# Row maxima of causal attention: full-height products with zero-padded keys, or 32-row groups of TensorE in bursts of three banks

## The chip, the cores and the metric

One NeuronCore of a Trainium2 chip runs the whole kernel. The metric is device time in microseconds (us) from the first to the last instruction of that core; lower is better. The engines are TensorE (PE; its weight loads are listed as PEld), VectorE (DVE), ScalarE (ACT), GpSimd (POOL) and SyncE (SP), each with its own in-order instruction queue, tied together by semaphores.

## What is computed

A transformer block on 2 sequences of 1024 tokens with width 512: a modulated layer norm, attention with 16 query heads of 32 channels over one shared key and value head, a residual, a second modulated layer norm, and a mixture of 64 experts with 8 chosen per token and a shared expert. Only the attention matters here:

```python
q = rmsnorm(apply_rope((x @ Wq.T).reshape(B, S, H, hd).transpose(0, 2, 1, 3), S), w_qn)
k = rmsnorm(apply_rope(x @ Wk.T, S), w_kn)                      # one key head, hd = 32
scores = jnp.einsum('bhqd,bkd->bhqk', q, k) * scale
scores = jnp.where(causal, scores, jnp.finfo(scores.dtype).min)
attn = jax.nn.softmax(scores, axis=-1)                          # needs each row's maximum
out = jnp.einsum('bhqk,bkd->bhqd', attn, v)
```

## The kernel before

The first half of the span is attention, the second half the experts. Attention goes through 16 tiles of 128 query rows, `t` = 0 to 15, eight to a sequence (`i = t % 8`). Every engine walks the same hand-written calendar: a loop over slots `m`, 16 slots to a tile, in which each stage of the work has a fixed slot (tables `AT`, `FIRST_AT` and so on). Within a slot PE does, in this order, `row_max` (L1082), `scores` (L1132, transposed scores of a 256-query chunk), `values` (L1147, probabilities times values, in 32-column groups of the array, four heads side by side), then stages of other tiles: `stack` (L1117), the projections (L1051, L1060), transposes (L1040, L1072, L1079), the output projection (L1177), router logits and more. DVE does `end_max`, then `row_max`, then the rest of its slot (rotation, splitting, residuals, routing).

The row maxima are a pass of their own: the scores of a tile are made once with "f32r" operands (one pass through the array) only to find each row's maximum, which is then put into the query operand as extra channels (`end_max`, `stack`), so that the exponentials later need no maximum. For tile `i` a head's scores have (i+1)·128 columns. They are cut into pieces, each of which fills one PSUM bank of 512 columns: up to 512 columns `heads_in(width)` heads share a bank (4, 2, 1, 1 heads for i = 0 to 3); over 512 columns each head has a bank of its first 512 columns, and the rest is shared by 4, 2, 1, 1 heads (i = 4 to 7). That makes 4, 8, 16, 16, 20, 24, 32 and 32 banks for i = 0 to 7, 304 over both sequences. Three banks (4, 5, 6) go round; the pieces are spread evenly over the tile's 16 slots.

The contraction is only 32 channels. Before the change, a query operand `qpT` holds four heads stacked on 128 partitions, and the keys stand in `kpad`: four copies, copy `j` non-zero on partitions 32j to 32j+31 alone. So each head is one 128-row product (L1092). The bank that holds the diagonal gets a causal bias through an identity product (L1096). `s_mm` counts finished banks, and DVE reduces each bank when it is there (L1610) and counts it in `s_max`; PE waits before it writes bank n until bank n−3 is reduced. `keys_out` on ACT fills `kpad` with four copies of 32 partitions (L817) after the key transpose (L1079). At the start DVE clears `kpad` (L1489). Full-array products of ones (L1032, `keep_warm`) fill some early gaps.

Of the kernel before, what the change touches and what calls it, by code (L numbers as in the profile page):

```python
# [6 lines left out]
H, HD = 16, 32  # L7
# [52 lines left out]
def build_program(nc, x, c_t, wmod, wq_t, wkv_t, wo_t, w_pre, w_qn, w_kn, router_t, e_bias,  # L60
# [11 lines left out]
    with ctx:  # L72
# [27 lines left out]


        att = ExitStack()
        kpad = sb(att, "kpad", [P, GH, S], f32r)
        qs = sb(att, "qs", [P, 2, H, QK])
        wq = sb(att, "wq", [P, KC, D])
        wkv = sb(att, "wkv", [P, KC, 2 * HD])
# [70 lines left out]
        nmax = sb(att, "nmax", [P, 2, H])  # L177
        seen = sb(att, "seen", [P, E])
        seen_b = sb(att, "seen_b", [P, E], bf16)
        steps = sb(att, "steps", [P, P, 4], f16)  # L180
# [169 lines left out]

            return min(GH, 512 // width)

        def pieces(i):

            width = (i + 1) * P
            if width <= 512:
                return H // heads_in(width)
            return H + H // heads_in(width - 512)

        def pieces_before(t):  # L360

            return sum(pieces(k % TPB) for k in range(t))

        def pieces_at(i, h):
            width = (i + 1) * P
            if width <= 512:
                k = heads_in(width)
                return [(h // k, h, k, 0, width)] if h % k == 0 else []
            k = heads_in(width - 512)
            found = [(h + h // k, h, 1, 0, 512)]  # L370
            if h % k == k - 1:
                found.append((h + h // k + 1, h + 1 - k, k, 512, width))
            return found

        def max_view(n, heads, width):

            bank = ps[:, MAX_BANK + n % MAX_BANKS, :].rearrange("p (a k) -> p a k", a=heads)
            return bank[:, :, 0:width]

        def keys(q):  # L380

# [145 lines left out]
        def _(sp):  # L527
# [51 lines left out]

            for t in range(CT * CLOSE):  # L580
                if t == CT * (CLOSE - 1):
                    sp.wait_ge(s_mm, pieces_before(NT))
# [160 lines left out]
        def _(act):  # L743
# [58 lines left out]
            def pack_out(t):  # L802
                act.wait_ge(s_pack, t + 1)
                if t >= 2:
                    act.wait_ge(s_mm, pieces_before(t - 1))
                act.activation(qpT[:, t % 2, :, :], ps[:, T_BANK, :].rearrange("p (g t) -> p g t", t=P), ACT.Copy)\
                   .then_inc(s_qp, 1)

            def keys_out(t):
                b, i = divmod(t, TPB)  # L810
                act.wait_ge(s_pack_k, t + 1)
                act.activation(kT[0:QK, b, i * P:i * P + P], ps[0:QK, T_BANK, 0:P], ACT.Copy)
                if t and i == 0:
                    act.wait_ge(s_mm, pieces_before(t))
                for j in range(GH):
                    r = slice(HD * j, HD * j + HD)
                    last = act.activation(kpad[r, j, i * P:i * P + P], ps[0:HD, T_BANK, 0:P], ACT.Copy)  # L817
                last.then_inc(s_packT, 1)

            def stack_out(t, q4):  # L820
# [207 lines left out]
        def _(pe):  # L1028
# [47 lines left out]
            def pack_keys(t):  # L1076
                keep_warm(("pack_keys", t))
                pe.wait_ge(s_qp, t + 1)
                pe.transpose(ps[0:QK, T_BANK, 0:P], ks[:, :], ident).then_inc(s_pack_k, 1)  # L1079

            def row_max(t, h):
                i = t % TPB  # L1082
                for n, first, heads, lo, hi in pieces_at(i, h):
                    if n == 0:
                        keep_warm(("row_max", t))
                        pe.wait_ge(s_packT, t + 1)
                    n += pieces_before(t)
                    if n >= MAX_BANKS:
                        pe.wait_ge(s_max, n - MAX_BANKS + 1)
                    view, diagonal = max_view(n, heads, hi - lo), hi == (i + 1) * P  # L1090
                    for a in range(heads):
# [28 lines left out]
            def scores(q, g, kt):  # L1120
                b, off, n = q // CPB, first_query(q, kt), step_of(q, g, kt)
                if g == 0 and kt == 0:
                    pe.wait_ge(s_qT, CT * (q + 1) * NG)
                for pr in range(2):
                    if wide_units(2 * n + pr) >= 4:
                        pe.wait_ge(s_exp, 2 * n + pr - 3)
                    elif wide_units(2 * n + pr) >= 2:
                        pe.wait_ge(s_max, pieces_before(NT))
# [356 lines left out]
        def _(dve):  # L1485

            dve.memset(ones_b[:, :], 1.0).then_inc(s_blank, 1)
            dve.memset(silu_c[:, :, :], 0.0).then_inc(s_blank, 1)
            dve.memset(kpad[:, :, :].bitcast(f32), 0.0)  # L1489
            dve.memset(ones[:, :], 1.0)  # L1490
            dve.memset(mhalf[:, :], -0.5)
            dve.memset(seen[:, :], 0.0)
# [89 lines left out]
            def split(t, n):  # L1582
# [30 lines left out]
            def end_max(t):  # L1613
                q_parts = qs[:, t % 2, :, :]
                dve.drain()
                if t % TPB >= 4:
                    dve.tensor_tensor(nmax[:, 0, :], nmax[:, 0, :], nmax[:, 1, :], ALU.min)
                    dve.drain()
                dve.tensor_copy(q_parts[:, :, 3 * HD].bitcast(f32r), nmax[:, 0, :])
                dve.drain()  # L1620
                dve.tensor_tensor(q_parts[:, :, 3 * HD + 1].bitcast(f32r), nmax[:, 0, :], q_parts[:, :, 3 * HD],
                                  ALU.subtract).then_inc(s_nmax, 1)
                dve.drain()

            def divide(q, g):
# [480 lines left out]
```

## Time and profile before

| | |
|---|---|
| time, median of 3 runs (lowest to highest) | 1232.77 us (1232.52 to 1236.47) |
| profiled execution, its own span | 1233.0 us |
| PE busy | 1168.1 us, 95% |
| DVE busy | 972.6 us, 79% |
| ACT busy | 762.0 us, 62% |
| POOL busy | 497.9 us, 40% |
| DVE maxima, L1610 | 304 instructions, 191.3 us |
| PE products of the maxima, L1092 | 384 instructions, 146.7 us |

Busy time is the union of an engine's instructions. A product's listed duration has the time in it that results need to leave the array, so that a chain of products overlaps itself: the rate is read from start to start, not from the mean duration. "PEclk" in the views of stretches is the clock granted to TensorE, as a share of full speed.

### The profile page before, as it was taken

How to read it: one execution, taken by the hardware profiler on the slowest of the kernel's cores; microseconds unless marked ns; L12 is line 12 of the kernel's file. 1: busy time of each engine (PE TensorE's matmuls, PEld its weight loads, DVE VectorE, ACT ScalarE, POOL GpSimd, SP SyncE). 2: the span in 40 equal slices, each digit the busy share in tenths (PEclk: the TensorE clock that was granted, in tenths of full speed). 3: DMA queues.
4: the chain of work that ended last, by engine and by line, in shares of the span. 5: the costliest groups of instructions: out<-in, count | busy, mean ns of one | idle time of the engine just before them, and what ended most of it. 6: DMA issues, size and time to landing. Idle time of an engine off the chain costs nothing.

```text
span 1233.0 us, 25541 instructions
## 1 busy us (share of the span) xinstructions
PE 1168.1 (95%) x8905; PEld 879.7 (71%) x8905; DVE 972.6 (79%) x1881; ACT 762.0 (62%) x1507; POOL 497.9 (40%) x375
## 2 busy tenths in 40 slices
PE   8988999999999988999999999999999999999996
PEld 4455556555565655555557899999999999999982
DVE  4678776756657888775767889899888999999976
ACT  3456555555664644455564477787777887777841
POOL 1122212102122111201100148887888778788740
PEclk9999999989999998999999999999999999999999
DMA  9570000000000000003004179999999999999988
GB/s 349 172 302 1 2 18 2 10 9 2 15 10 10 9 1 22 1 10 95 29 14 141 25 225 299 289 302 302 292 295 306 299 297 296 298 301 294 298 231 290
DMA packets 75167, 189.95 MB, mean 154 GB/s; under 512 B 11544, under 2 KB 12184, under 8 KB 74832
## 3 DMA queue, kind: packets, MB, share of 16 engines
q1 hardware_dynamic: 44704, 116.27, 28.0%
q0 software_dynamic: 28672, 71.32, 23.5%
q10 hardware_dynamic: 1712, 1.32, 0.3%
q8 instruction: 48, 0.79, 0.3%
q14 instruction: 31, 0.25, 0.1%
HBM read 136.36 MB, written 52.51 MB: 153 GB/s over the span
## 4 chain that ended last, share of the span: by engine, by line
PE 71%; DVE 13%; DVEq 4%; issue 3%; DMA 3%; ACT 3%; POOL 0%; SPq 0%; POOLq 0%; ACTq 0%
PE ps L1328 22%; PE ps L1367 12%; PE ps L1147 8%; PE ps L1314 5%; PE ps L1177 4%; PE ps L1132 4%; PE ps L1060 4%; PE ps L1092 4%; DVE nmax L1610 3%; PE ps L1117 2%; DMA acc_dram<-y,slots 1%; PE ps L1032 1%; PE ps L1164 1%; DMA wq<-in_wq_t 1%; PE ps L1195 1%
## 5 line engine op out<-in xcount | busy, mean ns | idle before, releaser
L730 POOL DMA_INDIRECT acc_dram<-y,slots x128 | 252.2, 1971 | 74.1 <-issue 47.9
L1610 DVE TENSOR_REDUCE nmax<-ps 128x1 f32<-128x512 f32 (+3 forms) x304 | 191.3, 656 | 95.3 <-PE ps L1096 52.4
L839 ACT ACTIVATE probs<-ps 128x512 f32<-128x512 f32 (+1 forms) x320 | 159.0, 554 | 87.2 <-PE ps L1132 86.3
L681 POOL TENSOR_SCALAR_AFFINE_SELECT probs<-probs 128x512 f32<-128x512 f32 x64 | 44.3, 691 | 376.7 <-ACT probs L839 376.6
L715 POOL DMA_INDIRECT xg<-h_dram,slots x128 | 130.7, 1021 | 84.4 <-DVE slots L1801 40.5
L1092 PE MATMUL ps<-kpad,qpT 128*128 128x512 f32 (+3 forms) x384 | 146.7, 450 | 15.5 <-DVE nmax L1610 13.4
L1328 PE MATMUL ps<-x_hi,e_gu_hi 128*112 128x256 f32 (+1 forms) x768 | 120.1, 278 | 0.0
L1132 PE MATMUL ps<-qT,kT 98*128 98x512 f32 (+1 forms) x320 | 115.1, 437 | 5.0 <-ACT probs L839 4.8
L1328 PE MATMUL ps<-x_hi,e_gu_lo 128*112 128x256 f32 (+1 forms) x768 | 119.6, 278 | 0.0
L1812 DVE TENSOR_TENSOR e_gu_lo<-e_gu,e_gu_hi 128x1408 fp32r<-128x1408 f32 x64 | 103.8, 1622 | 11.0 <-ACT e_gu_hi L960 9.9
L1328 PE MATMUL ps<-x_lo,e_gu_hi 128*112 128x256 f32 (+1 forms) x768 | 109.9, 279 | 0.0
L1328 PEld LDWEIGHTS ps<-x_hi,e_gu_hi 128*112 128x112 f32 (+1 forms) x768 | 105.7, 179 | 5.9
L1092 PEld LDWEIGHTS ps<-kpad,qpT 128*128 128x128 f32 x384 | 67.3, 195 | 50.3 <-DVE nmax L1610 25.4
L1328 PEld LDWEIGHTS ps<-x_hi,e_gu_lo 128*112 128x112 f32 (+1 forms) x768 | 100.8, 179 | 0.0
L1328 PEld LDWEIGHTS ps<-x_lo,e_gu_hi 128*112 128x112 f32 (+1 forms) x768 | 96.0, 179 | 0.0
L1812 DVE TENSOR_TENSOR x_lo<-ps,x_hi 128x1024 fp32r<-128x1024 f32 x72 | 88.1, 1224 | 2.9 <-ACT x_hi L937 1.9
L960 ACT ACTIVATE e_gu_hi<-e_gu 128x1408 fp32r<-128x1408 f32 x64 | 88.2, 1378 | 0.1
L1367 PE MATMUL ps<-e_d_hi,hid_hi 112*128 112x512 f32 (+1 forms) x256 | 85.9, 417 | 0.0
L937 ACT ACTIVATE x_hi<-ps 128x1024 fp32r<-128x1024 f32 x72 | 73.9, 1026 | 18.5 <-PE ps L1314 18.1
L1147 PE MATMUL ps<-probs,v_sb 128*32 128x256 f32 (+1 forms) x1280 | 83.4, 380 | 0.6 <-POOL probs L681 0.6
L1367 PE MATMUL ps<-e_d_hi,hid_lo 112*128 112x512 f32 (+1 forms) x256 | 80.8, 397 | 0.0
L1147 PE MATMUL ps<-probs,ones 128*32 128x256 f32 (+1 forms) x1280 | 79.4, 367 | 0.0
(238 smaller groups left out, 2375.1 us busy)
## 6 DMA issues: line engine op xcount, KB each, us to landing
e_gu<-in_gate_up SPq DMA_DIRECT2D x64, 704.0 KB, 7.3
e_d<-in_w_down SPq DMA_DIRECT2D x64, 224.0 KB, 4.7
acc_dram<-h SPq DMA_DIRECT2D x2, 4608.0 KB, 26.0
e_d<-in_w_down SPq DMA_DIRECT2D x64, 128.0 KB, 5.4
wmod_b<-in_wmod SPq DMA_DIRECT2D x2, 2048.0 KB, 22.0
xg<-h_dram SPq DMA_DIRECT2D x16, 256.0 KB, 7.0
acc_a<-acc_dram SPq DMA_DIRECT2D x8, 512.0 KB, 10.0
acc_b<-acc_dram SPq DMA_DIRECT2D x8, 512.0 KB, 7.7
```

Of the source, the lines that this page charges most:

```text
L715: pool.indirect_dma_start(out=xg[r][:, h, :], out_offset=None, in_=h2_dram, in_offset=bass.IndirectOffsetOnAxis(ap=slots[:, at:at + 1], ax ...
L730: pool.indirect_dma_start(out=acc_dram[a], out_offset=bass.IndirectOffsetOnAxis(ap=slots[:, at:at + 1], axis=0), in_=y[e % 2][:, h, :], in ...
L839: act.activation(probs[:, n % PROBS, 2 * pr:2 * pr + 2, off:CW], unit_bank(2 * n + pr)[:, :, off:CW], ACT.Exp).then_inc(s_exp, 1)
L937: act.activation(x_hi[p][:, :, :].rearrange(flat), pair(0).rearrange(flat), ACT.Copy).then_inc(s_xa, 1)
L960: act.activation(e_gu_hi[p][:, :, :].rearrange(flat), e_gu[p][:, :, :].rearrange(flat), ACT.Copy)\
L1092: last = pe.matmul(view[:, a, :], qpT[:, t % 2, (first + a) // GH, :], kpad[:, (first + a) % GH, lo:hi], start=(a == 0), stop=(a == heads ...
L1132: pe.matmul(unit_bank(2 * n + pr)[:, :, off:CW], kT[0:QK, b, kt * P:kt * P + P], qT[q % 2][0:QK, head:head + 2, off:CW], start=True, stop= ...
L1147: last = pe.matmul(ps[HD * j:HD * j + HD, PV_BANK, at + off:at + CW], v_sb[:, b, kt, :] if at == 0 else ones[:, :], probs[:, (n + kt % 2) ...
L1328: last = pe.matmul(dst, w[:, cc, col:col + wide], rows_t[:, cc, :], start=(k == 0 and cc == 0), stop=(k == 2 and cc == KC - 1))
L1367: last = pe.matmul(ps[:, 6 + h, :], left[:, h * P:(h + 1) * P], w, start=(k == 0), stop=(k == len(products) - 1))
L1610: dve.tensor_reduce(nmax[:, 1 if lo else 0, first:first + heads], max_view(n, heads, hi - lo), AX.X, ALU.max, negate=True).then_inc(s_max, 1)
L1812: return dve.tensor_tensor(dst[:, :, :].rearrange(flat), whole[:, :, :].rearrange(flat), hi[:, :, :].bitcast(f32).rearrange(flat), ALU.sub ...
```

## The change

The keys are now one tile `kq`, with the 32 key channels repeated on all four groups of 32 partitions. DVE writes four copies of the keys side by side into `ks4`, and a second 128-column transpose turns them, so that ACT moves them with one copy of 128 partitions in place of four of 32. A head's product takes only its own 32 rows of `qpT` and `kq`. A bank now holds heads with the same place `j` in their group of four, so that neighbouring banks use different row groups. Banks are handled in bursts of three: PE issues the first head of each of the three banks, then the second heads, and so on, then the diagonal biases of the three, and counts `s_mm` once for the burst. DVE waits for the burst, and then reduces and counts each bank by itself. Before PE writes bank k of a burst, it waits until the bank in the same place has been reduced (`drained`). Tiles i = 0 to 7 have 2, 3, 6, 6, 7, 8, 11 and 11 bursts (54 to a sequence, 108 in all); burst n of N stands in the first slot h with h ≥ 16·n/N, rounded down: for 11 bursts these are slots 0, 1, 2, 4, 5, 7, 8, 10, 11, 13 and 14. The clearing of `kpad` is gone. All waits that counted pieces now count bursts (PE's progress) or banks (DVE's).

```diff
-        kpad = sb(att, "kpad", [P, GH, S], f32r)
+        kq = sb(att, "kq", [P, S], f32r)
+        ks4 = sb(att, "ks4", [P, GH, HD])
...
+        def max_banks(i):
+            found = []
+            for part, (lo, hi) in enumerate(max_parts(i)):
+                k = heads_in(hi - lo)
+                for n in range(H // k):
+                    q, j = divmod(n, GH)
+                    found.append((part * H + n * k, [GH * (q * k + a) + j for a in range(k)], lo, hi))
             return found
+        def bursts(i):
+            banks = max_banks(i)
+            return [banks[n:n + MAX_BANKS] for n in range(0, len(banks), MAX_BANKS)]
+        def bursts_at(i, h):
+            found = bursts(i)
+            return [(n, banks) for n, banks in enumerate(found) if n * H // len(found) == h]
...
 keys_out (ACT):
-                for j in range(GH):
-                    r = slice(HD * j, HD * j + HD)
-                    last = act.activation(kpad[r, j, i * P:i * P + P], ps[0:HD, T_BANK, 0:P], ACT.Copy)
+                last = act.activation(kq[:, i * P:i * P + P], ps[:, T_BANK, P:2 * P], ACT.Copy)
...
 pack_keys (PE):
+                pe.transpose(ps[:, T_BANK, P:2 * P], ks4[:, :, :].rearrange("p j d -> p (j d)"), ident)\
+                  .then_inc(s_pack_k, 1)
...
 row_max (PE):
-                for n, first, heads, lo, hi in pieces_at(i, h):
+                for n, banks in bursts_at(i, h):
                     if n == 0:
                         keep_warm(("row_max", t))
                         pe.wait_ge(s_packT, t + 1)
-                    n += pieces_before(t)
-                    if n >= MAX_BANKS:
-                        pe.wait_ge(s_max, n - MAX_BANKS + 1)
-                    view, diagonal = max_view(n, heads, hi - lo), hi == (i + 1) * P
-                    for a in range(heads):
-                        last = pe.matmul(view[:, a, :], qpT[:, t % 2, (first + a) // GH, :],
-                                         kpad[:, (first + a) % GH, lo:hi], start=(a == 0),
-                                         stop=(a == heads - 1 and not diagonal))
-                    if diagonal:
-                        last = pe.matmul(view[:, :, hi - lo - P:hi - lo], ident_b[:, :],
-                                         bias_b[:, :].unsqueeze(1).to_broadcast([P, heads, P]), start=False, stop=True)
+                    for a in range(max(len(heads) for _, heads, _, _ in banks)):
+                        for k, (_, heads, lo, hi) in enumerate(banks):
+                            if a < len(heads):
+                                if a == 0 and drained(t, n, k):
+                                    pe.wait_ge(s_max, drained(t, n, k))
+                                g, j = divmod(heads[a], GH)
+                                r = slice(HD * j, HD * j + HD)
+                                last = pe.matmul(max_view(k, 1, hi - lo)[:, a, :], qpT[r, t % 2, g, :], kq[r, lo:hi],
+                                                 start=(a == 0), stop=(a == len(heads) - 1 and hi != (i + 1) * P))
+                    for k, (_, heads, lo, hi) in enumerate(banks):
+                        if hi == (i + 1) * P:
+                            last = pe.matmul(max_view(k, 1, hi - lo)[:, :, hi - lo - P:hi - lo], ident_b[:, :],
+                                             bias_b[:, :].unsqueeze(1).to_broadcast([P, len(heads), P]), start=False, stop=True)
                     last.then_inc(s_mm, 1)
...
-            dve.memset(kpad[:, :, :].bitcast(f32), 0.0)
...
 split (DVE):
+                    dve.tensor_copy(ks4[:, :, :].bitcast(f32r), t1[:, H, :].unsqueeze(1).to_broadcast([P, GH, HD]))
...
 row_max (DVE):
-                for n, first, heads, lo, hi in pieces_at(i, h):
-                    n += pieces_before(t)
-                    dve.wait_ge(s_mm, n + 1)
-                    dve.tensor_reduce(nmax[:, 1 if lo else 0, first:first + heads], max_view(n, heads, hi - lo), AX.X, ALU.max,
-                                      negate=True).then_inc(s_max, 1)
+                for n, banks in bursts_at(i, h):
+                    dve.wait_ge(s_mm, bursts_before(t) + n + 1)
+                    for k, (first, heads, lo, hi) in enumerate(banks):
+                        dve.tensor_reduce(nmax[:, first:first + len(heads)], max_view(k, 1, hi - lo), AX.X, ALU.max,
+                                          negate=True).then_inc(s_max, 1)
```

`end_max` reads the maxima in their new order of heads; it has the same three small operations.

## Rows read from the trace of the kernel before

**Rows 1.** The page's busy line and its chain that ended last.
```profile
PE 1168.1 (95%) x8905; PEld 879.7 (71%) x8905; DVE 972.6 (79%) x1881; ACT 762.0 (62%) x1507; POOL 497.9 (40%) x375
...
PE 71%; DVE 13%; DVEq 4%; issue 3%; DMA 3%; ACT 3%; POOL 0%; SPq 0%; POOLq 0%; ACTq 0%
```

**Rows 2.** Stretches: length; busy (instructions) of PE, PEld, DVE, ACT, POOL; PEclk, DMA, GB/s.
```profile
93.00:182.00 89.00, 80.83 (x602) 51.17 (x600) 70.42 (x142) 49.03 (x117) 20.58 (x20) 0.96 0.02 7
182.00:267.00 85.00, 80.57 (x634) 49.16 (x635) 59.62 (x120) 44.37 (x102) 13.38 (x13) 0.94 0.02 7
...
386.00:491.00 105.00, 93.30 (x686) 58.66 (x684) 93.07 (x214) 50.97 (x120) 20.13 (x19) 0.97 0.04 12
491.00:567.00 76.00, 71.88 (x610) 43.26 (x608) 59.63 (x123) 39.72 (x84) 10.05 (x12) 0.98 0.03 9
```

**Rows 3.** Groups by line: busy, mean ns; idle before them, and releasers.
```profile
L1610 DVE TENSOR_REDUCE nmax<-ps 128x1 f32<-128x512 f32 (+3 forms) x304 | 191.3, 656 | 95.3 <-PE ps L1096 52.4 <-PE ps L1092 40.1 <-issue 0.8
```

**Rows 4.** Who waited for whom, PE alone, 30 to 600 us: total, times, longest.
```profile
PE ps L1092 <- DVE nmax L1610: 13.4, 18, 1.8
...
PE ps L1117 <- DVE qs L1621: 4.1, 10, 0.9
PE ps L1092 <- ACT kpad L817: 1.8, 4, 1.0
```

**Rows 5.** Order of time in tile 7: start, length, engine, line, operation.
```profile
241.45 0.60 PE L1189 MATMUL ps<-con,h 128*128 128x128 f32 x4
...
241.81 0.71 PE L1092 MATMUL ps<-kpad,qpT 128*128 128x512 f32 x2
...
242.36 0.23 PE L1096 MATMUL ps<-bias_b,ident_b 128*128 128x128 bf16 x1
242.37 0.31 PEld L1132 LDWEIGHTS ps<-qT,kT 98*128 98x128 f32 x2
242.40 0.71 PE L1132 MATMUL ps<-qT,kT 98*128 98x512 f32 x2
```

**Rows 6.** Order of time: narrow products of tile 0, and a run of L1032.
```profile
39.73 0.52 PEld L1092 LDWEIGHTS ps<-kpad,qpT 128*128 128x128 f32 x4 [0.84 <-issue]
...
35.55 1.67 PE L1032 MATMUL ps<-ones_b 128*128 128x512 bf16 x7
```

**Rows 7.** Order of time: from full array to 32-column groups and back.
```profile
244.28 0.23 PE L1096 MATMUL ps<-bias_b,ident_b 128*128 128x128 bf16 x1
244.44 0.59 PEld L1147 LDWEIGHTS ps<-probs,v_sb 128*32 128x32 f32 x16
244.45 1.07 PE L1147 MATMUL ps<-probs,v_sb 128*32 128x256 f32 x16
...
245.33 1.05 PE L1147 MATMUL ps<-probs,ones 128*32 128x256 f32 x16
...
246.31 0.30 PEld L1060 LDWEIGHTS ps<-wq,hT 128*128 128x128 f32 x2 [0.41 <-issue]
```

**Rows 8.** Order of time: a wait for a bank, and values at the lower clock.
```profile
227.77 0.68 DVE L1610 TENSOR_REDUCE nmax<-ps 128x1 f32<-128x512 f32 x1
227.91 0.19 PEld L1092 LDWEIGHTS ps<-kpad,qpT 128*128 128x128 f32 x1 [1.81 <-DVE nmax L1610]
...
231.48 1.94 PE L1147 MATMUL ps<-probs,v_sb 128*32 128x256 f32 x16
...
233.19 1.27 PE L1147 MATMUL ps<-probs,ones 128*32 128x256 f32 x16
```

**Rows 9.** Stretches, columns as in rows 2, at two falls of the clock.
```profile
223.40:226.80 3.40, 3.01 (x30) 1.81 (x19) 3.00 (x7) 1.79 (x4) 0.35 (x1) 1.00 0.00 0
226.80:230.20 3.40, 1.82 (x10) 1.21 (x10) 3.40 (x8) 1.71 (x4) 0.38 (x2) 1.00 0.00 0
230.20:233.60 3.40, 3.40 (x24) 1.75 (x28) 3.21 (x6) 0.89 (x3) 1.90 (x3) 0.51 0.02 5
...
499.90:503.30 3.40, 1.85 (x13) 1.30 (x12) 3.21 (x7) 1.22 (x4) 2.95 (x2) 1.00 0.00 0
503.30:506.70 3.40, 3.40 (x28) 1.76 (x31) 1.94 (x5) 1.69 (x3) 0.89 (x1) 0.50 0.00 0
```

**Rows 10.** Order of time: key copies of tile 0, clearing of `kpad`, first load.
```profile
35.92 1.08 ACT L817 ACTIVATE kpad<-ps 32x128 fp32r<-32x128 f32 x4
...
2.00 3.47 DVE L1489 MEMSET kpad<- 128x4096 f32 x1 [0.80 <-issue]
...
2.80 13.23 DMA wq<-in_wq_t
```

More of the change, by code:

```diff
@@ L102, in build_program @@
         att = ExitStack()
-        kpad = sb(att, "kpad", [P, GH, S], f32r)
+        kq = sb(att, "kq", [P, S], f32r)
+        ks4 = sb(att, "ks4", [P, GH, HD])
+        hole = sb(att, "hole", [P, (GH - 1) * S - GH * HD])
         qs = sb(att, "qs", [P, 2, H, QK])
@@ L176, in build_program @@
         rr = sb(att, "rr", [P, H + 1])
-        nmax = sb(att, "nmax", [P, 2, H])
+        nmax = sb(att, "nmax", [P, 2 * H])
         seen = sb(att, "seen", [P, E])
@@ L351, in heads_in, with max_parts @@
             return min(GH, 512 // width)
-        def pieces(i):
+        def max_parts(i):
             width = (i + 1) * P
[L356 to L372, printed above, removed]
-            return found
@@ L375, in max_view @@
-        def max_view(n, heads, width):
-            bank = ps[:, MAX_BANK + n % MAX_BANKS, :].rearrange("p (a k) -> p a k", a=heads)
-            return bank[:, :, 0:width]
+            return [(lo, min(width, lo + 512)) for lo in range(0, width, 512)]
+        def max_banks(i):
[5 more added lines that the diff above has]
+                    found.append((part * H + n * k, [GH * (q * k + a) + j for a in range(k)], lo, hi))
+            return found
@@ new lines, in bursts, with bursts_before, banks_before, drained @@
+        def bursts(i):
+            banks = max_banks(i)
+            return [banks[n:n + MAX_BANKS] for n in range(0, len(banks), MAX_BANKS)]
+        def bursts_before(t):
+            return sum(len(bursts(k % TPB)) for k in range(t))
+        def banks_before(t):
+            return sum(len(max_banks(k % TPB)) for k in range(t))
+        def drained(t, n, k):
+            sizes = [len(burst) for s in range(t + 1) for burst in bursts(s % TPB)[:n if s == t else None]]
+            while sizes and sizes[-1] <= k:
+                sizes.pop()
+            return sum(sizes[:-1]) + k + 1 if sizes else 0
@@ new lines, in bursts_at, with by_head, max_view @@
+        def bursts_at(i, h):
+            found = bursts(i)
+            return [(n, banks) for n, banks in enumerate(found) if n * H // len(found) == h]
+        def by_head(flat, width):
+            k = heads_in(width)
+            return flat.rearrange("p (q j a) -> p q a j", j=GH, a=k)
+        def max_view(bank, count, width):
+            heads = heads_in(width)
+            return ps[:, MAX_BANK + bank:MAX_BANK + bank + count, :].rearrange("p b (a k) -> p (b a) k", a=heads)[:, :, 0:width]
@@ L581, in _ @@
                 if t == CT * (CLOSE - 1):
-                    sp.wait_ge(s_mm, pieces_before(NT))
+                    sp.wait_ge(s_mm, bursts_before(NT))
                     sp.wait_ge(s_sc, 2 * steps_before(CLOSE))
@@ L804, in pack_out @@
                 if t >= 2:
-                    act.wait_ge(s_mm, pieces_before(t - 1))
+                    act.wait_ge(s_mm, bursts_before(t - 1))
                 act.activation(qpT[:, t % 2, :, :], ps[:, T_BANK, :].rearrange("p (g t) -> p g t", t=P), ACT.Copy)\
@@ L813, in keys_out @@
                 if t and i == 0:
-                    act.wait_ge(s_mm, pieces_before(t))
-                for j in range(GH):
-                    r = slice(HD * j, HD * j + HD)
-                    last = act.activation(kpad[r, j, i * P:i * P + P], ps[0:HD, T_BANK, 0:P], ACT.Copy)
+                    act.wait_ge(s_mm, bursts_before(t))
+                last = act.activation(kq[:, i * P:i * P + P], ps[:, T_BANK, P:2 * P], ACT.Copy)
                 last.then_inc(s_packT, 1)
@@ L1078, in pack_keys @@
                 pe.wait_ge(s_qp, t + 1)
-                pe.transpose(ps[0:QK, T_BANK, 0:P], ks[:, :], ident).then_inc(s_pack_k, 1)
+                pe.transpose(ps[0:QK, T_BANK, 0:P], ks[:, :], ident)
+                pe.transpose(ps[:, T_BANK, P:2 * P], ks4[:, :, :].rearrange("p j d -> p (j d)"), ident)\
+                  .then_inc(s_pack_k, 1)
             def row_max(t, h):
                 i = t % TPB
-                for n, first, heads, lo, hi in pieces_at(i, h):
+                for n, banks in bursts_at(i, h):
                     if n == 0:
@@ L1127, in scores @@
                     elif wide_units(2 * n + pr) >= 2:
-                        pe.wait_ge(s_max, pieces_before(NT))
+                        pe.wait_ge(s_max, banks_before(NT))
                     elif 2 * n + pr >= 2:
@@ L1606, in row_max @@
                 i = t % TPB
-                for n, first, heads, lo, hi in pieces_at(i, h):
-                    n += pieces_before(t)
-                    dve.wait_ge(s_mm, n + 1)
-                    dve.tensor_reduce(nmax[:, 1 if lo else 0, first:first + heads], max_view(n, heads, hi - lo), AX.X, ALU.max,
-                                      negate=True).then_inc(s_max, 1)
+                for n, banks in bursts_at(i, h):
[3 more added lines that the diff above has]
+                                          negate=True).then_inc(s_max, 1)
             def end_max(t):
+                i = t % TPB
                 q_parts = qs[:, t % 2, :, :]
                 dve.drain()
-                if t % TPB >= 4:
-                    dve.tensor_tensor(nmax[:, 0, :], nmax[:, 0, :], nmax[:, 1, :], ALU.min)
+                (lo, hi), *rest = max_parts(i)
+                top = by_head(nmax[:, 0:H], hi - lo)
+                for lo, hi in rest:
+                    dve.tensor_tensor(top, top, by_head(nmax[:, H:2 * H], hi - lo), ALU.min)
                     dve.drain()
-                dve.tensor_copy(q_parts[:, :, 3 * HD].bitcast(f32r), nmax[:, 0, :])
+                columns = [q_parts[:, :, 3 * HD + n].rearrange("p (q a j) -> p q a j", a=top.shape[2], j=GH) for n in range(2)]
+                dve.tensor_copy(columns[0].bitcast(f32r), top)
                 dve.drain()
-                dve.tensor_tensor(q_parts[:, :, 3 * HD + 1].bitcast(f32r), nmax[:, 0, :], q_parts[:, :, 3 * HD],
-                                  ALU.subtract).then_inc(s_nmax, 1)
+                dve.tensor_tensor(columns[1].bitcast(f32r), top, columns[0], ALU.subtract).then_inc(s_nmax, 1)
                 dve.drain()
```

## The prediction, written before the changed kernel was run

> **What bounds the kernel now.** I read the page first. TensorE is busy 95% of the span, VectorE 79%, and the chain that ended last lies on PE for 71% and on DVE for 13% [rows 1]. The expert half is untouched by the diff, so I looked only at attention, tile by tile, in the view of stretches. In tiles 3 to 5, 6 and 7, and 14 and 15 PE is busy nine tenths of the time or more and DVE seven to eight tenths; in tiles 11 to 13 both stand at 89% (93.3 and 93.1 of 105 us) [rows 2]. So PE's own in-order queue sets the pace, with DVE close behind in one stretch of 105 us. The reader should hold that against the DVE group of the maxima: it sat idle 95 us waiting for PE's banks [rows 3], whereas PE itself stood still for a reduced bank 13.4 us [rows 4]. Time taken off PE is worth nearly its full length; time taken off DVE is worth little; any new wait of PE costs its full length, because scores, values and projections of all other tiles queue behind it. The median of the runs, 1232.77, and the profiled span, 1233.0, are the same within 0.3 us, so I sum against 1233. About 0.3% (3.7 us) is what a measurement of this kernel can tell from no change.
>
> **Part 1, the products themselves.** Column time first. A head of tile i streams (i+1)·128 columns: 36·128·16·2 = 147,456 columns. Seven products of 512 columns take 1.67 us with a tail of about 0.38, so 0.215 us each [rows 6]; the column time is 62 us. Three at a time would make it 21, if products in different row groups run side by side. No row of before shows row groups. The nearest row shows column groups: 16 products of L1147 start at 244.45 and the next 16 at 245.33, 0.055 us apiece, where each one alone has 256 columns in two passes, 0.215 us: four do run together [rows 7]. I take the same for row groups.
>
> But the same rows show the price of changing the split of the array. Without a change, the weights of L1132 begin to load as the bias product starts (242.37 against 242.36) [rows 5]. With one, the weights for L1147 wait 0.16 us after the bias product starts (244.44 against 244.28), and on the way back those for L1060 start only at 246.31, when the last values product, of 245.33 + 1.05 = 246.38, has all but ended [rows 7]. A full-width weight load takes 0.11 us ((0.52 − 0.19)/3) [rows 6], and it no longer hides behind the product before. I put entering a burst at 0.20 us, leaving it for the short bf16 load of the bias at 0.11, and leaving it for a full-width load (bursts without a diagonal) at 0.20.
>
> Now per three banks, on PE's queue. Before: in tile 7 two banks, one with a diagonal, take 242.40 − 241.81 = 0.59 us [rows 5]; I split that as 0.22 without and 0.37 with the diagonal, the bias costing more than its 0.05 because the next weight load is exposed. Three banks are 0.65 and 1.08. For 384 columns with a diagonal 0.90, for two heads of 256 about 1.03, for four heads of 128 (weight loads of 0.11 each, then a 0.22 bias) 1.98. After: 0.20 + 0.23 + 0.20 = 0.64 without a diagonal; 0.20 + 0.23 + 0.11 + three biases of 0.055 + 0.08 exposed load = 0.80 with one; 0.75, 0.90 and 1.43 for the other three. With the number of banks (4, 8, 16, 16, 20, 24, 32, 32) that is 46 us before and 39.5 after for one sequence, so **−13 us** for both. The changes of split eat most of the 41 that the overlap would give. Bounds: no price for a change of split at all, 108·0.35 = 38 us more gain, −51; no overlap at all, +41, so +28. I stay at −13, nearest to what L1147 shows.
>
> The Trainium skill, TensorEngine Tiling (Array Packing), Key Properties, says that changing the tiling mode drains the TensorE while changing the tile does not; that speaks against this change, and the L1147 rows agree with it (0.16 us to the next weights where it is otherwise 0.01). The same page under Theoretical Speedup allows up to 4× for contractions of 32 rows; by that alone the part would be −41 us, not −13.
>
> **Part 2, keys.** ACT's four copies take 1.08 us [rows 10], one takes about 0.28; but PE stood waiting on them only 1.8 us in all [rows 4], with as much again in weight loads: −3. The second transpose adds 16 products of about 0.11 us on PE: +2. The extra copy on DVE, about 0.2 us × 16, lies in DVE's idle time, except in tiles 11 to 13, where it costs 0.6 at most. The clearing of `kpad`, 3.47 us from 2.00, ends at 5.5 us while the chain waits for the `wq` load until 16 us [rows 10]: nothing. Together **−1** (−4 to +2).
>
> **Part 3, end of a tile.** The last burst stands in slot 13 or 14, before the change the last bank stood in 14 or 15, so `end_max` no longer comes right behind two maxima. PE waits 4.1 us for it now at L1117 [rows 4], more with the weight loads: **−4** (−10 to 0).
>
> **Part 4, the new wait.** Before, PE could fill bank n while n−1 and n−2 were still to be reduced. Now the third bank of a burst needs the third maximum of the burst before. Behind PE's wait stand the slot's scores and values. After the burst's last product 0.25 us pass until DVE has its count, then three maxima of 0.68 [rows 8]: the last bank is free 2.3 us or more later. With two or more slots between bursts PE has 3.5 us or more of other work and does not notice. In tiles 6, 7, 14 and 15, 11 bursts stand in 16 slots and six of the ten steps are to the very next slot. Slots last 85/32 = 2.6 and 76/32 = 2.4 us there [rows 2]; less 0.6 for the burst PE has 1.8 to 2.0 us, so it waits 0.3 to 0.5, and more where DVE has other work in front: the wait of 1.8 us at 227.91 is such a one [rows 8]. 24 such steps at 0.6: **+15** (0 to +30). DVE's other results come up to 1.4 us later behind a block of three maxima; the slack of the calendar hides that, except in tiles 2, 3 and 11 to 13, and this is in the upper bound.
>
> **Part 5, the clock.** The granted clock falls to 1.2 GHz now and then: 0.96, 0.94, 0.97 and 0.98 in the mean of the stretches of rows 2, which is 3.6 + 5.1 + 3.2 + 1.5 = 13 us of clock, or some eight falls as long as the one shown. Ahead of the two shown PE was thinly used: 1.82 us busy of 3.40, then 0.51 of full speed; 1.85 of 3.40, then 0.50 [rows 9]. A fall costs: 16 values products need 1.71 us (231.48 to 233.19) [rows 8] against 0.88 [rows 7], half the length of a fall, so up to 1.7 us, some of which is spent waiting anyway: 1.3. The change takes two thirds of the maxima's column time off PE without shortening the tile by as much, in just the tiles where the clock already falls. I estimate one further fall for each of the ten tiles 2 to 7 and 12 to 15, **+14** (0 to +35).
>
> **Sum.** −13 − 1 − 4 + 15 + 14 = +11: 1233 + 11 = **1244 us**.
>
> **The rivals.** *Faster: the overlap counts and the clock holds.* If the lower clock does not come more often, because PE is fed as densely as now, and the waits in adjacent slots lie in DVE's idle 95 us, the sum is −13 − 1 − 4 + 3 = −15, 1218. If changing to row groups is also somewhat cheaper than to column groups, up to 10 us more go, 1208. For it speak the high share of PE in every stretch and DVE's idle time; against it the falls that are there already. Chance 0.25, for 1208 to 1229.
>
> *Much faster: row groups overlap in full and changing to them is free.* The column time falls by 41 us, and with parts 2 to 4 the time is 1233 − 41 − 5 + 15 = 1202; L1147's two gaps speak against it. Chance 0.08. The skill's speedup rule, taken alone, would end here.
>
> *No difference.* Waits and falls half as dear as I put them: −18 + 15, within 1229 to 1237. Chance 0.15.
>
> *Much slower: row groups do not run side by side*, or the waits compound because DVE, at 89% in tiles 11 to 13, becomes the bound and idles once per burst for PE's 0.9 us refill. Without overlap 41 us come back and the clock falls no oftener: 1233 + 28 − 5 + 15 = 1271. With compounding, 21 bursts × 0.9 = 19 us on top of 1244, 1263. Against the first speaks L1147; against the second that DVE has other work between bursts that covers a refill. Chance 0.10 beyond 1262.
>
> **How the numbers follow.** The forecast, slower by several us up to 1262, has 0.42; faster 0.25 and much faster 0.08; same 0.15; much slower 0.10. The sign turns on parts 4 and 5 being 18 us together. Range: from 1208, leaving out the case in which changes of split are free, to 1268, leaving out the dearest part of the last rival. The forecast's own range is 1237 to 1262. Chances: faster 0.33, same 0.15, slower 0.52.
>
> **What the profile after would show.** Right: products of different row groups starting a few ns apart; gaps of about 0.2 us in weight loads on entering a burst; the busy time of L1092's successor well under 100 us; more stretches at 0.5 of the clock in tiles 2 to 7 and 12 to 15; waits of PE on L1610's successor above the 13.4 of now, mostly in tiles 6, 7, 14 and 15; DVE's idle time ahead of the maxima still near 90. Wrong: no more falls than now (part 5 goes, and the result is about 1230), weight loads of a row group starting before the previous split's products end (part 1 is −40), or waits that stay where they are.

## The result, and the profile after

The changed kernel takes 1246.29 us (median, 1243.51 to 1250.71), 1.0116 of the kernel before (95% interval 1.0088 to 1.0144): 13.7 us slower, where 11 were forecast. The profiled execution spans 1241.8 us and is the fastest of the four runs.

The page after, busy line and chain, in answer to rows 1:

```profile
PE 1174.5 (95%) x8921; PEld 858.8 (69%) x8921; DVE 968.9 (78%) x1896; ACT 745.3 (60%) x1459; POOL 493.3 (40%) x375
...
PE 74%; DVE 13%; ACT 3%; DVEq 3%; issue 3%; DMA 2%; POOL 0%; SPq 0%; POOLq 0%; ACTq 0%
```

Still a TensorE kernel. The stretches of the same tiles (3 to 5, 6 and 7, 11 to 13, 14 and 15; columns as in rows 2):

```profile
94.00:185.00 91.00, 82.22 (x605) 47.22 (x605) 69.17 (x143) 46.36 (x107) 20.22 (x20) 0.89 0.01 4
185.00:270.00 85.00, 82.02 (x648) 44.56 (x646) 60.04 (x124) 43.08 (x98) 13.24 (x13) 0.96 0.02 7
...
385.00:495.00 110.00, 95.88 (x703) 55.12 (x702) 93.45 (x216) 50.59 (x115) 20.84 (x20) 0.94 0.03 9
495.00:576.00 81.00, 75.67 (x606) 41.52 (x607) 60.23 (x123) 35.67 (x76) 10.04 (x12) 0.90 0.02 8
```

Against [rows 2] the last two are longer by 5 us each and the first by 2, and the clock column is lower in three of four: 0.89 for 0.96, 0.94 for 0.97, 0.90 for 0.98.

The maxima's groups of instructions (busy, mean ns; idle before, releasers), of the changed kernel:

```profile
L1637 DVE TENSOR_REDUCE nmax<-ps 128x1 f32<-128x512 f32 (+3 forms) x304 | 183.0, 655 | 97.5 <-PE ps L1123 78.9 <-PE ps L1119 17.7
L1119 PE MATMUL ps<-kq,qpT 32*128 32x512 f32 (+3 forms) x384 | 75.4, 436 | 10.3 <-DVE nmax L1637 7.2 <-ACT kq L840 0.5
```

The products' busy time is 75 us where it was 147, and DVE's idle time stays at 98 (95 in [rows 3]). One burst in order of time, PE's products and then its weight loads, in answer to rows 5 and 7:

```profile
253.99 0.72 PE L1222 MATMUL ps<-rw,h2T 128*128 128x64 f32 x5
254.64 0.50 PE L1119 MATMUL ps<-kq,qpT 32*128 32x512 f32 x3
255.07 0.34 PE L1123 MATMUL ps<-bias_b,ident_b 128*128 128x128 bf16 x3
255.22 0.71 PE L1159 MATMUL ps<-qT,kT 98*128 98x512 f32 x2
...
254.64 0.19 PEld L1119 LDWEIGHTS ps<-kq,qpT 32*128 32x128 f32 x3
255.07 0.17 PEld L1123 LDWEIGHTS ps<-bias_b,ident_b 128*128 128x128 bf16 x3 [0.25 <-issue]
```

Three products of 512 columns take 0.50 us together, where two at full height took 0.71 [rows 5]: row groups do run side by side, and their three weight loads do too (0.19 for three). And the split is paid for: the weights of L1119 start only at 254.64, when the router's products are nearly through (253.99 + 0.72 = 254.71), those of the bias at 255.07, when the burst is (254.64 + 0.50 = 255.14). From 254.64 to L1159 it is 0.58 us; with the 0.2 of the entry, which lies ahead of 254.64, that is close to the 0.80 of the sum.

Who waited for whom, weight loads only (38 to 640 us), before and then after; a weight load shows waits that the tail of the product before hides in PE's own line. Each line has total, times and longest:

```profile
PEld ps L1092 <- DVE nmax L1610: 25.4, 47, 1.9
PEld ps L1117 <- ACT qT L828: 12.3, 26, 0.8
PEld ps L1117 <- DVE qs L1621: 8.2, 11, 1.3
...
```

```profile
PEld ps L1119 <- DVE nmax L1637: 31.6, 67, 3.2
PEld ps L1144 <- ACT qT L851: 19.8, 25, 1.4
PEld ps L1144 <- DVE qs L1652: 2.2, 3, 1.6
```

The wait for the maxima grew by 6 us, the wait for the query parts shrank by 6, and a wait the prediction did not have grew by 7.5: the stack products for ACT's query copy. PE's own line has 7.2 us for the maxima, where it had 13.4 [rows 4]. The weight loads' wait for the maxima in tiles 6 and 7, then 14 and 15, before and then after:

```profile
PEld ps L1092 <- DVE nmax L1610: 5.3, 12, 1.8
...
PEld ps L1092 <- DVE nmax L1610: 5.4, 12, 1.9
```

```profile
PEld ps L1119 <- DVE nmax L1637: 8.1, 19, 0.8
...
PEld ps L1119 <- DVE nmax L1637: 10.1, 25, 1.0
```

So 7.5 us came in the four tiles that part 4 named, in the weight loads; PE's own waits there fell by 3. In order of time, changed kernel, tile 3:

```profile
98.29 0.60 ACT L851 ACTIVATE qT<-ps 98x512 fp32r<-98x512 f32 x1
98.94 0.28 PEld L1144 LDWEIGHTS ps<-con,qs 128*98 128x98 f32 x3 [0.94 <-ACT qT L851]
```

A tile's query is stacked in four steps in four successive slots, and each needs ACT's 0.60 us copy of the step before. Before the change a bank or two of maxima stood in most slots and could cover the copy; now some slots have none. That this is what made the wait longer is not shown: an experiment below with one bank to a burst has most of the growth too.

Last, the clock over the whole span, before and then after:

```profile
core 0: 1233.0 us, clock 0.984
```

```profile
core 0: 1241.8 us, clock 0.971
```

The clock is full or half in every stretch that the trace records, so the time at half is 2 × (1 − clock) × span: 39 us before and 72 after in the profiled executions. A single execution says little here, as every run has its own clock: over the four runs of the changed kernel it is 72, 77, 80 and 97 us, mean 82; over 35 runs of the kernel before it is 25 to 44, mean 34. In the mean it is 48 us more.

### The profile page after: what moved, and what is told of

Same layout as the page of the kernel before. It is cut to its first block, busy times and chain, and to the rows that moved or that the text cites. A ratio compares the mean times of both kernels' runs of the same rounds, so it can differ in the third digit from the quotient of the medians.

```text
span 1241.8 us, 25540 instructions
## 1 busy us (share of the span) xinstructions
PE 1174.5 (95%) x8921; PEld 858.8 (69%) x8921; DVE 968.9 (78%) x1896; ACT 745.3 (60%) x1459; POOL 493.3 (40%) x375
## 4 chain that ended last, share of the span: by engine, by line
PE 74%; DVE 13%; ACT 3%; DVEq 3%; issue 3%; DMA 2%; POOL 0%; SPq 0%; POOLq 0%; ACTq 0%
PE ps L1355 22%; PE ps L1394 12%; PE ps L1174 8%; PE ps L1341 5%; PE ps L1083 4%; PE ps L1159 4%; PE ps L1204 4%; PE ps L1119 4%; DVE nmax L1637 4%; PE ps L1144 2%; PE ps L1123 1%; PE ps L1055 1%; ACT probs L862 1%; DMA wq<-in_wq_t 1%; PE ps L1074 1%
## 5 line engine op out<-in xcount | busy, mean ns | idle before, releaser
L755 POOL DMA_INDIRECT acc_dram<-y,slots x128 | 248.4, 1940 | 77.0 <-issue 51.3
L1637 DVE TENSOR_REDUCE nmax<-ps 128x1 f32<-128x512 f32 (+3 forms) x304 | 183.0, 655 | 97.5 <-PE ps L1123 78.9
L1159 PE MATMUL ps<-qT,kT 98*128 98x512 f32 (+1 forms) x320 | 121.2, 456 | 5.1 <-ACT probs L862 4.7
L1119 PE MATMUL ps<-kq,qpT 32*128 32x512 f32 (+3 forms) x384 | 75.4, 436 | 10.3 <-DVE nmax L1637 7.2
L1174 PE MATMUL ps<-probs,ones 128*32 128x256 f32 (+1 forms) x1280 | 83.7, 382 | 0.0
L1159 PEld LDWEIGHTS ps<-qT,kT 98*128 98x128 f32 x320 | 53.5, 196 | 38.5 <-ACT probs L862 20.5
```

What stands on the lines that cost most here:

```text
L755: pool.indirect_dma_start(out=acc_dram[a], out_offset=bass.IndirectOffsetOnAxis(ap=slots[:, at:at + 1], axis=0), in_=y[e % 2][:, h, :], in ...
L1119: last = pe.matmul(max_view(k, 1, hi - lo)[:, a, :], qpT[r, t % 2, g, :], kq[r, lo:hi], start=(a == 0), stop=(a == len(heads) - 1 and hi ! ...
L1174: last = pe.matmul(ps[HD * j:HD * j + HD, PV_BANK, at + off:at + CW], v_sb[:, b, kt, :] if at == 0 else ones[:, :], probs[:, (n + kt % 2) ...
L1637: dve.tensor_reduce(nmax[:, first:first + len(heads)], max_view(k, 1, hi - lo), AX.X, ALU.max, negate=True).then_inc(s_max, 1)
```

## Experiments

Each is compared with the kernel before on the same chip (medians 1231.0 to 1232.4 us). Two experiments that ran on different chips are best compared by their ratios. "Half" is the time at half clock worked out as above, in the mean of a kernel's runs; lines of the profile show one run.

**Bundling, with full-height products.**

```diff
 (changed kernel)
-   pe.matmul(max_view(k, 1, hi - lo)[:, a, :], qpT[r, t % 2, g, :], kq[r, lo:hi], ...)
+   pe.matmul(max_view(k, 1, hi - lo)[:, a, :], qpT[:, t % 2, g, :], kpad[:, j, lo:hi], ...)
```

> Bursts of three banks with their counts and waits, but full-height products on zero-padded keys and the old way of copying keys, so row groups, the second transpose and their effect on the clock are undone. My sum (waits +15, earlier end of a tile -4): 1244 us, stretches at half clock about as long in all as before (31 us in attention). Rival, the waits cost nothing and the whole loss is row groups and clock: 1229 to 1233 us.

The old key copies are back too. Measured: 1249.19 us, ratio 1.0141 (1.0124 to 1.0158), half 49 us. That is 5 above my 1244 and far from the rival. Bursts of three with their new order of banks cost 17 us, and the changed kernel is 3 us better than this one, with 32 us more at half clock. Its weight loads:

```profile
PEld ps L1116 <- DVE nmax L1634: 29.8, 75, 3.0
PEld ps L1141 <- ACT qT L851: 20.0, 24, 1.3
PEld ps L1141 <- DVE qs L1649: 3.2, 2, 1.7
```

The three waits of the changed kernel are all here, so they come from bundling and order and not from row groups.

**Two and one to a burst,** full height, going round the three banks:

```diff
-   return [banks[n:n + MAX_BANKS] for n in range(0, len(banks), MAX_BANKS)]
+   return [banks[n:n + BURST] for n in range(0, len(banks), BURST)]     # BURST 2, 1
...
-   pe.wait_ge(s_max, drained(t, n, k))
+   pe.wait_ge(s_max, ring(t, n, k) - MAX_BANKS + 1)
```

> As e1_full (full-height products, no row groups), but bursts of two banks that go round the three banks, so that PE may fill a third bank while two wait. If the 17 us of e1_full come from bundling three banks (PE's other work is left bare in the slots without a burst, and PE and DVE are tied tighter), two to a burst should lose less than half: 1235 to 1241 us, and PE's wait at the stack products for ACT's query copy falls from 12 us towards the 5 of before. Rival, they come from the new order of heads or from counting at all: 1246 to 1250 us as before.

> As e5_full2 with one bank to a burst: only the order of heads and banks differs from the kernel before. Bundling theory: 1229 to 1236 us. Rival, the order of heads and banks costs: 1240 us or more.

Measured: 1240.82 us for two (1.0074, 1.0052 to 1.0096), 1233.83 for one (1.0030, 1.0013 to 1.0047). Both lie in my ranges. So one, two and three to a burst cost 3, 10 and 17 us over the kernel before: 14 of the 17 are bundling, about 3 the new order of heads and banks. The stack products' wait for ACT is 17.6, 19.5 and 20.0 us, against 12.3 before: 5.3 of its 7.5 us come with the new order, and it does not fall as expected; it alone is not the cause. Half is 31 us with one and 32 with two, so the 7 us between them are not the clock. What grows from one to two is the wait for the maxima (first one to a burst, then two):

```profile
PEld ps L1121 <- DVE nmax L1639: 23.5, 46, 2.1
```

```profile
PEld ps L1121 <- DVE nmax L1639: 38.9, 56, 3.0
```

From two to three it falls back to 29.8 while the time rises by 8 us. Half rises from 32 to 49 us, which at the price found below (0.34 us of time for each us at half clock) is about 6 of the 8; the rest I can't assign to one wait.

**Row groups in bursts of two.** The same edit on the changed kernel.

> The changed kernel with 32-row groups, but bursts of two in a ring of three banks: 152 in place of 108 changes to row groups and only two products side by side. By my prices of a change of split (0.20 in, 0.11 or 0.20 out) row groups then cost 8 us of PE per sequence more than full height, and the clock some 7: e5_full2 + 22, about 1260 us. Rival, a change of split is cheap: row groups are no dearer than full height, within 5 us of e5_full2.

Measured: 1270.70 us, 1.0327 (1.0304 to 1.0351), 30 us above the same bursts at full height.

```profile
core 0: 1267.1 us, clock 0.956
```

Half is 114 us against 32. The time is 10 us above the 1260 I expected, and the split between causes did not hold: at 0.34 the 82 us more at half clock are 28 of the 30. That leaves some 2 us for row groups in pairs at an even clock, where I had put 16.

**No overlap.** Banks sorted by row group within a tile, so that a burst's banks mostly share one.

```diff
+   found.sort(key=lambda bank: (bank[2], bank[1][0] % GH))
    return found
```

> The changed kernel, with the banks of a tile ordered so that those of one burst mostly have the same row group and can't run side by side; changes of split, waits and column count are the same. If the overlap is worth its 41 us of column time on PE's queue: 1246 + 41 less some falls of the clock that no longer happen, 1273 to 1287 us. Rival, the bursts stand in time that PE waits anyway: under 1262 us.

Measured: 1269.05 us, 1.0305 (1.0285 to 1.0324), 23 us above the changed kernel. Below what I expected and above the rival. One error was mine: 16 banks in bursts of three are not all of one group (14 steps where 6 would do, not 16), so the column time lost is about 28 us, not 41. Half is 84 us against 82, so the clock has no part in it. Most of the 28 shows in the time: the overlap is real and lies on PE's path.

**The price of a change of split.** Full-height bursts with one small 32-row product ahead of each.

```diff
+   if a == 0 and k == 0:
+       pe.matmul(ps[:, MAX_BANK, 0:64], qpT[0:HD, t % 2, 0, :], kpad[0:HD, 0, 0:64], start=True, stop=True)
```

> As e1_full, with one 32-row product of 64 columns ahead of each of the 108 bursts, written into the burst's first bank and overwritten: it adds two changes of split to a burst and next to no column time. By my prices 0.2 + 0.2 + 0.03 us each, 108 times, less what lies in waits: 1249 + 30 to 46, 1279 to 1295 us. Rival, a change of split costs only the weight load of 0.11 us: 1260 to 1265 us.

Measured: 1274.80 us, 1.0357 (1.0297 to 1.0417), 26 us above bursts without it, at the same half (47 and 49 us): 0.24 us for two changes and the small product itself. Between the two theories; the load alone would have made 11 to 16. The weight loads of the small product and of the burst wait for the maxima for 17.7 and 7.7 us, where they waited 29.8 without it:

```profile
PEld ps L1116 <- DVE nmax L1637: 17.7, 28, 2.6
...
PEld ps L1119 <- DVE nmax L1637: 7.7, 27, 0.4
```

So some 4 us, 0.04 to a burst, are seen to be hidden in these waits. That makes 0.28, not the 0.40 of my price; whether more is hidden in other waits is open.

**Products of ones ahead of the bursts** of tiles 4 to 7 and 12 to 15 (74 bursts), after the wait for the burst's first bank; in the changed kernel, in full-height bursts, and two of them in the changed kernel.

```diff
+   if a == 0 and k == 0 and i >= 4:
+       pe.matmul(ps[:, MAX_BANK, :]..., ones_b[:, :], ones_b..., start=True, stop=True)
```

> The changed kernel, with one full-array product of ones (512 columns) ahead of each burst in tiles 4 to 7 and 12 to 15, written into the burst's first bank once it is free and overwritten by the burst. 74 products of 0.22 us and an exposed weight load, 16 to 20 us of PE. If falls of the clock come from a thinly used array and cost 14 us: half-clock time goes from about 61 us in attention back to 30 or less and the time is 1246 to 1254 us. Rival, the falls have another cause: half-clock time stays at 50 to 60 us, 1262 to 1266 us.

> As e1_full, with the same 74 products of ones as in e4_warm. It tells how much of them lies in PE's waits for the second and third bank. In e4_warm they cost only 2 us. If that was because 14 to 18 us of them lie in waits, they cost 2 us here too, 1249 to 1252 us. If it was because they bring back the clock, which full-height bursts lose less, they cost more here: 1255 to 1262 us.

> As e4_warm, with two products of ones ahead of each burst of these tiles. Clock theory: half-clock time in attention goes on falling, below 40 us; time 1252 to 1258 us, as the second product no longer lies in a wait and one fall less gives back 1.3 us each. If the clock does not answer to such products: half-clock time 45 to 60 us, 1262 us or more.

Measured: 1248.03 us (1.0123, 1.0100 to 1.0146), 1.7 above the changed kernel (0.9 by the ratios); 1250.12 in full-height bursts (1.0149, 1.0099 to 1.0198), 0.9 above them; 1251.71 with two (1.0154, 1.0101 to 1.0208). In tile 4 one such product does what it was put there for. The same stretch, changed kernel and then with it:

```profile
116.00:119.40 3.40, 3.04 (x13) 2.16 (x13) 2.93 (x5) 1.52 (x4) 0.22 (x1) 0.51 0.00 0
119.40:122.80 3.40, 2.71 (x17) 1.33 (x19) 3.05 (x8) 1.24 (x3) 1.30 (x2) 0.50 0.00 0
```

```profile
116.00:119.40 3.40, 2.33 (x16) 1.51 (x17) 3.24 (x6) 2.03 (x5) 0.63 (x1) 1.00 0.00 0
119.40:122.80 3.40, 3.40 (x48) 2.29 (x48) 3.31 (x9) 1.32 (x4) 1.09 (x2) 1.00 0.00 0
```

In the second of these PE handles 48 products in place of 17. Over the whole kernel half falls too: from 82 us to 53 with one product and to 41 with two (30 to 53 in its four runs), and from 49 to 37 in full-height bursts. With two products the profiled run is the slowest of the four and has 53 us, hardly less than the 55 of the profiled run with one; the other three have 30, 38 and 45. So the clock does answer to such products: the times of one and of two lie in or beside the ranges of the clock theory (1246 to 1254 and 1252 to 1258) and far from the 1262 of its rivals, though half did not fall as low as 30 with one.

The product of ones is cheap for two reasons, and these runs do not part them well. At 0.34 the 29 us less at half clock give back 10 of its 16 to 20 us. In full-height bursts the clock gives back only 4, and yet the product costs 0.9 us there, which fell on the side of hidden waits in its own test; but that ratio is known only to 6 us either way. The weight loads of the product and of the burst wait for the maxima, in the changed kernel (product L1119, burst L1123) and then in full-height bursts (product L1117, burst L1120):

```profile
PEld ps L1119 <- DVE nmax L1641: 10.6, 18, 3.1
...
PEld ps L1123 <- DVE nmax L1641: 9.8, 25, 0.8
```

```profile
PEld ps L1120 <- DVE nmax L1638: 14.1, 43, 0.4
...
PEld ps L1117 <- DVE nmax L1638: 11.2, 19, 2.7
```

That is 11 us less than the 31.6 without the product, and some 4 less than the 29.8.

**One maximum instruction per burst.**

```diff
-   for k, (first, heads, lo, hi) in enumerate(banks):
-       dve.tensor_reduce(nmax[:, first:first + len(heads)], max_view(k, 1, hi - lo), ...).then_inc(s_max, 1)
+   dve.tensor_reduce(nmax[:, first:first + count * len(heads)], max_view(k, count, hi - lo), ...).then_inc(s_max, count)
```

> The changed kernel, with one maximum instruction and one count for all banks of a burst that have the same shape. A block of three banks is then reduced about 0.3 us sooner, so PE's wait in adjacent slots is shorter. If the waits cost 15 us as in my sum: 1238 to 1242 us. Rival, PE hardly waits for maxima: 1244 to 1248 us, no change against 1246.

> As e3_one (one maximum instruction for a burst) with the 74 products of ones of e4_warm. PE's wait for the maxima is 26 us there and all three banks come free at once, so the products lie ahead of nothing that is waited for any more and cost their 16 us less the clock's gain: 1248 to 1256 us. If the clock's gain outweighs them: under 1243 us.

Measured: 1242.85 us, 1.0114 (1.0067 to 1.0161), and with the products of ones 1250.95, 1.0158 (1.0108 to 1.0208). The first is 3.4 us better than the changed kernel by the medians and the same by the ratios, so it decides nothing. Its weight loads wait 41.2 us for the maxima, ten more, and PE's own line has 25.6 for 7.2: a bank that is counted with its neighbours is not free sooner. Here the products of ones cost 5 us by the ratios and 8 by the medians, and the time is in the range expected.

**The last burst in slot 15.**

```diff
-   ... if n * H // len(found) == h]
+   ... if (H - 1 if n == len(found) - 1 else n * H // len(found)) == h]
```

> The changed kernel with the last burst of each tile moved from slot 13 or 14 to slot 15. If the earlier end of a tile was worth its 4 us (16 tiles, PE's stack products waiting for the maxima put into the query): 1249 to 1254 us, and the weight loads of the stack products wait for DVE's query parts 8 us or more in place of 2.2. Rival, it was worth nothing: 1244 to 1248 us.

In tiles 0 and 1 of each sequence the last burst stood in slots 8 and 10, which the text ahead of the run and the prediction overlook, so there it moves further. Measured: 1268.39 us, 1.0280 (1.0251 to 1.0308), 22 us above the changed kernel (20 by the ratios), outside both ranges, and by neither theory's mechanism: the stack products' weight loads wait 2.8 us for the query parts, not 8.

```profile
PEld ps L1120 <- DVE nmax L1638: 22.8, 53, 2.4
...
PEld ps L1145 <- DVE qs L1653: 2.8, 3, 1.5
```

```profile
core 0: 1271.6 us, clock 0.947
```

The weight loads' wait for maxima shrank, but PE's own doubled. The changed kernel, then this one:

```profile
PE ps L1119 <- DVE nmax L1637: 7.2, 11, 3.0
```

```profile
PE ps L1120 <- DVE nmax L1638: 14.4, 15, 2.2
```

What changed most is the clock: half 127 us against 82, 45 more for 20 to 22 us of time. If all of that time were the clock, it would be 0.44 to 0.49 us for each us at half clock, but the wait above shows that another cost hides in it.

**The price of the clock.** A price with less beside it comes from runs of one and the same kernel, where no line of code differs and the clock does. The changed kernel's four runs go from 1243.51 us at a clock of 0.971 to 1250.71 at 0.961: 7.2 us for 25 more at half, 0.28. All 94 runs of the thirteen changed kernels and of the kernel before, each taken against the mean of its own kernel and chip, give a slope of **0.34 us for each us at half clock** (0.13 to 0.49 in single kernels). A run that is slow for another reason could have more time at half clock because of it, so this is how time and clock go together, and not proof of what drives what.

None of the twelve kernels beats the one before.

## Why the prediction was right, and where it was not

With the price of 0.34 and half in the mean of the runs, the 13.7 us come apart so. Bursts of three cost 17 us (full height), of which 14 us more at half clock are 5, so 12 without the clock. The changed kernel is 3 us faster than that with 32 us more at half clock, worth 11, so row groups and the key copies give −14. The clock costs 48 × 0.34 = 16. These are 12 − 14 + 16 = 14. The terms hang on the price: with 0.27 they are 13, −12 and 13, with 0.46 they are 11, −18 and 22. By the profiled executions alone (33 us more at half clock) the clock would be 11.

- **Products (part 1, −13) and keys (part 2, −1):** together about −14, as forecast. The overlap and the price of changing the split were read from column groups [rows 7] and carried over to row groups as they were, and that held. At an even clock the price comes out three times, after hiding: (40 saved − 14) / 108 = 0.24 us a burst for threes, 0.24 for the small 32-row product, (31 saved + 2) / 152 = 0.22 for pairs. These are estimates from the column times (62 us at full height, 22 in threes, 31 in pairs). The sum had 0.31 to 0.40 for the same. Two slips did not matter: the products after come to 38.8 us for a sequence and not 39.5, and the bound of −51 is more than the 41 that the overlap can give.
- **The drain at a change of split.** The Trainium skill, TensorEngine Tiling (Array Packing), Key Properties, says that a change of mode drains TensorE. The burst above agrees with it, and so does the small 32-row product (0.24 us after hiding). The 4× that the Trainium skill gives on the same page under Theoretical Speedup, which alone led to 1202 us, is out: the products did run side by side, but −14 came and not −41.
- **End of a tile (part 3, −4):** the wait for the query parts fell from 8.2 to 2.2 us in the weight loads, as said. Moving the last burst did not bring it back, so that wait is not what the last slot costs.
- **The new wait (part 4, +15):** the sum of parts 3 and 4, +11, stands against about 12 measured, and that is in part luck. PE's own wait for the maxima was to rise above 13.4 us, and fell to 7.2. In the tiles named the weight loads' wait rose by 7.5, half of the 15. The step that failed is the picture of one wait in adjacent slots. The cost is spread: half of that wait, the new order of heads and banks (3 us), more waiting for ACT's query copy (+7.5 us in the weight loads, 5.3 of them with the new order), and a remainder that is not assigned.
- **The clock (part 5, +14):** about 16, by the profiled executions 11. In attention the profiled run has 61 us at half clock for 31, nine more falls of the length shown in [rows 9] where ten were said, most of them in the tiles named. The number of ten was a guess, and the mean of the four runs has some 14. The price of 1.3 us a fall is 0.38 for each us at half clock, and 0.34 was measured.
- **The rivals:** "faster" needed the clock to hold, and it did not. "No difference" needed waits and falls to cost 15 us; bundling and the clock cost 28. "No overlap" is ruled out by the burst itself and by the sorted banks. In tiles 11 to 13 the weight loads' wait for the maxima went from 8.7 to 7.0 us, so nothing compounded there.

The blocks come out within 2 us of the forecast at a price of 0.34, which is closer than that price is known. Inside part 4 the terms were wrong and made up for each other.

## What to carry to other kernels

Packing small products into row groups pays only if enough columns run between two changes of the array's split: here going in and out cost about 0.24 us a burst after hiding, three products of 512 columns saved 0.43 and paid, and two saved 0.215 and did not. Work that is bundled to make such packs is also taken from the slots where it covered other engines' latencies, so look in the view of waits, weight loads included, for who was covered by it. And a TensorE that does the same work in less streaming time may be given the lower clock: read the clock's mean over the span next to the time, before the waits are blamed, and read it for every run: two runs of one kernel differed by up to 36 us at half clock here (59 and 95 us, one maximum instruction per burst).

## What the runs showed of the hardware that was not expected

Weight loads of different row groups overlap: three full-width ones took 0.19 us together, where four into the full array took 0.52 [rows 6]. The clock answered to the placing of the work: moving the last burst of each tile to slot 15, by one or two slots in most tiles and with no work added, raised the time at half clock from 82 to 127 us in the mean of the runs. Taking row groups in pairs in place of full-height pairs raised it from 32 to 114. Why the one placing brings so many more falls is open.
